# Routing weights spread in three transfers per half, and the last row's gate copies moved from the scalar to the vector engine

## The reference

```python
scores = sigmoid(xt @ gate_w.T)
_, idx = top_k(scores + gate_b, 4)
w = take_along_axis(scores, idx); w = w / sum(w) * 2.5
comb = zeros((T, 16)).at[arange(T)[:, None], idx].add(w)     # the routing weights
def expert_body(y, (w13_e, w2_e, c_e)):
    gate, up = split(xt @ w13_e.T)                            # 64 columns each
    return y + c_e[:, None] * ((silu(gate) * up) @ w2_e.T)
y = scan(expert_body, 0, (w13, w2, comb.T)) + shared_expert(xt)
x = layernorm(x + y)
```

## Time and profile before

| | |
|---|---|
| time, median of 3 runs | 1407.15 us (1401.17 to 1414.5) |
| the profiled execution | 1402.87 us |
| its span, first to last instruction | 1401.1 us |
| busy: DVE, PE, ACT, POOL | 995.9, 891.7, 561.5, 84.2 us |
| chain that ended last | DVE 36%, PE 26%, issue 14%, ACT 11%, DMA 8%, SPq 4% |
| of the chain, DMA big<-comb_rows | 3% |
| TensorE clock granted, mean | 0.783 of full speed |

### The profile page before, as it was taken

The page is one execution under the profiler, slowest core; times in us unless marked ns, Lnnn a source line. Parts: engine busy times, 40 slices in busy tenths (PEclk is TensorE's granted clock), DMA queues, the critical chain, the costliest instruction groups (busy, mean ns, idle before and its releaser), DMA issues.

```text
span 1401.1 us, 29222 instructions
## 1 busy us (share of the span) xinstructions
PE 891.7 (64%) x11808; PEld 538.8 (38%) x11808; DVE 995.9 (71%) x2294; ACT 561.5 (40%) x1259; POOL 84.2 (6%) x56
## 2 busy tenths in 40 slices
PE   4655756786467587787457586787457576471554
PEld 2433535454234254454224254454324254240122
DVE  5456563567699987576699987566699986344985
ACT  3232332555643332565642332555643331455310
POOL 0000000020000000020000000020000000030630
PEclk8656767699768789699768789688767788686897
DMA  4110010311222210311223210311232210302410
GB/s 144 32 39 18 25 40 11 69 36 36 71 75 77 69 32 18 69 36 35 71 76 77 68 32 18 62 36 36 72 75 77 69 32 10 68 1 62 118 63 8
DMA packets 84823, 72.20 MB, mean 52 GB/s; under 512 B 24528, under 2 KB 63440, under 8 KB 84496
## 3 DMA queue, kind: packets, MB, share of 16 engines
q1 hardware_dynamic: 84688, 70.34, 19.2%
HBM read 66.51 MB, written 3.80 MB: 50 GB/s over the span
## 4 chain that ended last, share of the span: by engine, by line
DVE 36%; PE 26%; issue 14%; ACT 11%; DMA 8%; SPq 4%; POOL 0%; DVEq 0%; POOLq 0%; ACTq 0%
PE bank L720 6%; DVE SG L1739 5%; DMA big<-comb_rows 3%; PE bank L547 3%; SPq L484 3%; PE bank L752 2%; DVE Y L1832 2%; DVE XP L1752 2%; PE bank L878 2%; ACT relu_s L1031 2%; DVE CV L1752 2%; DVE bank L1739 1%; DMA RB<-rows_bounce 1%; DVE ml L1472 1%; DVE big L1727 1%
## 5 line engine op out<-in xcount | busy, mean ns | idle before, releaser
L720 PE MATMUL bank<-onehot,tparts 128*32 128x256 bf16 x3840 | 136.9, 303 | 56.7 <-DVE onehot L1518 54.0
L720 PEld LDWEIGHTS bank<-onehot,tparts 128*32 128x32 bf16 x3840 | 111.2, 106 | 91.2 <-issue 81.2
L878 PE MATMUL bank<-XP,CO 128*128 128x512 f32 x128 | 82.7, 780 | 57.8 <-DVE XP L1750 33.3
L1739 DVE TENSOR_TENSOR_SCAN SG<-big 128x512 f32<-128x512 f32 x96 | 111.7, 1204 | 0.9
L1220 ACT ACTIVATE big<-DEL,Aneg 128x512 f32<-128x512 f32 x96 | 63.8, 715 | 100.8 <-DVE SG L1739 94.9
L878 PE MATMUL bank<-CV,CO 128*128 128x512 f32 x128 | 79.2, 750 | 34.8 <-DVE CV L1752 22.8
L1031 ACT ACTIVATE relu_s<-bank,nml 128x192 f32<-128x192 f32 (+1 forms) x128 | 52.8, 425 | 110.4 <-DVE nml L1477 110.4
L1472 DVE TENSOR_REDUCE ml<-bank 128x2 f32<-128x384 f32 (+1 forms) x64 | 33.7, 568 | 65.6 <-PE bank L655 34.9
L752 PE MATMUL bank<-GT,QBD 128*32 128x32 f32 x3072 | 56.2, 208 | 33.3 <-DVE G L1527 23.4
L1518 DVE TENSOR_SCALAR onehot<-ib,CO 128x1024 bf16<-128x1024 f16 x160 | 69.9, 480 | 10.3 <-PE bank L720 8.6
L1084 ACT ACTIVATE GT<-bank 128x256 f32<-128x256 f32 x64 | 24.5, 383 | 129.7 <-PE bank L720 129.6
(11 more groups left out here) (307 smaller groups left out, 1979.2 us busy)
## 6 DMA issues: line engine op xcount, KB each, us to landing
BC<-bc_rows SPq DMA_DIRECT2D x128, 256.0 KB, 4.2
ib<-idx_rows SPq DMA_DIRECT2D x64, 256.0 KB, 4.0
big<-comb_rows SPq DMA_DIRECT2D x8, 1024.0 KB, 9.9
rows_bounce<-RO SPq DMA_DIRECT2D x256, 8.5 KB
W<-w SPq DMA_DIRECT2D x1, 2818.0 KB, 15.3
RB<-rows_bounce SPq DMA_DIRECT2D x16, 136.0 KB, 2.1
X<-x SPq DMA_DIRECT2D x4, 256.0 KB, 2.8
out<-CV SPq DMA_DIRECT2D x4, 256.0 KB, 2.3
```

What stands on the lines that cost most here:

```text
L720: m = mm(bank[2 + c % 2][32 * bb:32 * bb + 32, 256 * kind:256 * kind + 256], tparts[:, kt, part, 32 * kind:32 * kind + 32], onehot[:, n % ...
L878: mm(bank[5 + j][:, :], ident, hC[(n - 1) % 2][:, j, :], start=(n == 1), stop=(n == DS)).then_inc(ysum.sem, ysum.up())
L1739: m = dve.tensor_tensor_scan(state, decay, dBu[:, n % 2, j, :], 0.0, ALU.mult, ALU.add)
```

## The change

The two loads of `CB` per row become six: for pairs 0 and 1 (both halves, 256 KB each), for pairs 2 and 3 (256 KB each), and for pairs 4 to 7 (512 KB each), in this order, with the same packets of 2 KB. Each of the three parts has its own semaphore. POOL waits at steps 1 and 2 for the first part, at 3 and 4 for the second, from 5 on for the third. In the last row alone, ACT no longer copies the gate to `GU_turn`; DVE does it, behind a wait for `gm_ok` (ACT's relu on the same bank) and, as ACT did, for `hu_ok` of the step that had the buffer.

```diff
--- before.py
+++ after.py
@@ -338,6 +338,8 @@
         ct_ps = signal("comb_t_in_psum", 1)
         ct_sb = signal("comb_t_in_sbuf", 1)
         ct_st = signal("comb_stored", 1, 16)
+        cb_first = signal("routing_weights_spread_first_pairs", 2, 16)
+        cb_next = signal("routing_weights_spread_next_pairs", 2, 16)
         cb_sb = signal("comb_spread", 2, 16)
         ga_ps = signal("gate_in_psum", 9)
         up_ps = signal("up_in_psum", 9)
@@ -499,9 +501,10 @@
                 sp.wait_ge(ct_sb.sem, ct_sb.at(b, 1))
                 sp.dma_start(comb_rows, CT[:, :]).then_inc(ct_st.sem, ct_st.up())
                 sp.wait_ge(ct_st.sem, ct_st.at(b, 1))
-                for e in range(2):
-                    src = comb_rows.rearrange("(p e) t -> e p t", e=2)[e].unsqueeze(0).to_broadcast([64, NE // 2, L])
-                    sp.dma_start(CB[64 * e:64 * e + 64, :, :], src).then_inc(cb_sb.sem, cb_sb.up())
+                for lo, hi, part in ((0, 2, cb_first), (2, 4, cb_next), (4, NE // 2, cb_sb)):
+                    for e in range(2):
+                        src = comb_rows.rearrange("(p e) t -> e p t", e=2)[e][lo:hi].unsqueeze(0).to_broadcast([64, hi - lo, L])
+                        sp.dma_start(CB[64 * e:64 * e + 64, lo:hi, :], src).then_inc(part.sem, part.up())
                 for _ in range(EXPERT_PHASES - 2 + NORM_PHASES + SCAN_IN_PHASES - 4):
                     yield
                 sp.wait_ge(xd_sb.sem, xd_sb.at(b, 1))
@@ -1156,9 +1159,10 @@
                     if k >= T:
                         act.wait_ge(sg_ok.sem, sg_ok.at(b, k - T + 1))
                     clamped(bank[k0][0:rows, :], SGk[0:rows, 0, :], gm_ok)
-                    if k >= 3:
-                        act.wait_ge(hu_ok.sem, hu_ok.at(b, k - 2))
-                    A(GU_turn[k % 3][0:rows, :], bank[k0][0:rows, :], ACT.Copy).then_inc(gx_ok.sem, gx_ok.up())
+                    if not alone:
+                        if k >= 3:
+                            act.wait_ge(hu_ok.sem, hu_ok.at(b, k - 2))
+                        A(GU_turn[k % 3][0:rows, :], bank[k0][0:rows, :], ACT.Copy).then_inc(gx_ok.sem, gx_ok.up())
                     yield
                     act.wait_ge(gm_ok.sem, gm_ok.at(b, k + 1))
                     sigmoid_logs(SGk[0:rows, 0, :])
@@ -1291,7 +1295,8 @@
                     yield
                 for k in range(1, 9):
                     pool.wait_ge(ga_used.sem, ga_used.at(b, k + 1))
-                    pool.wait_ge(cb_sb.sem, cb_sb.at(b, 2))
+                    spread = cb_first if k <= 2 else cb_next if k <= 4 else cb_sb
+                    pool.wait_ge(spread.sem, spread.at(b, 2))
                     GUk = GU_turn[k % 3]
                     pool.tensor_tensor(GUk, GUk, CB[:, k - 1, :], ALU.mult).then_inc(ht_ok.sem, ht_ok.up())
                     yield
@@ -1660,6 +1665,11 @@
                         hidden(k - lag)
                     if k >= 1:
                         yield
+                    if alone:
+                        dve.wait_ge(gm_ok.sem, gm_ok.at(b, k + 1))
+                        if k >= 3:
+                            dve.wait_ge(hu_ok.sem, hu_ok.at(b, k - 2))
+                        CP(GU_turn[k % 3][0:rows, :], bank[k0][0:rows, :]).then_inc(gx_ok.sem, gx_ok.up())
                     dve.wait_ge(gx_ok.sem, gx_ok.at(b, k + 1))
                     dve.wait_ge(up_ps.sem, up_ps.at(b, k + 1))
                     TT(GU_turn[k % 3][0:rows, :], GU_turn[k % 3][0:rows, :], bank[k0 + 1][0:rows, :], ALU.mult).then_inc(ga_used.sem, ga_used.up())
```

## The result

| | before | after |
|---|---|---|
| median, runs | 1407.07 us, 4 (1401.17 to 1414.5) | 1389.95 us, 4 (1385.9 to 1398.89) |
| ratio, 95% interval | | 0.989, 0.9849 to 0.993 |
| the profiled execution; its span | 1402.87; 1401.1 us | 1398.89; 1397.1 us |
| mean granted clock of it | 0.783 | 0.774 |

The changed kernel is faster by 1.1%. The forecast was 1390 us. Two later sets gave 1388.49 against 1406.18 and 1390.41 against 1402.74 us.

The account below looks back on a forecast made before the run. The prediction saw waits on each row's routing-weight loads, with ACT setting the pace afterwards in the last row. Gains of 11.0 us (last row) and 4.4 us (woven rows), 15.4 us from a level of 1405, gave 1390 us, range 1380 to 1402.

Parts of the forecast that it names:

- Step 1: Last row: first weights land 5.0 us after the first issue, so POOL starts 7.95 us sooner.
- Step 2: Last row: PE returns at full clock, POOL to relu of step 4 takes 5.12 us, gaining 1.85 us.
- rival B: Last row: the clock falls as before, so the kernel takes 1391.5 us; chance 0.10.
- Step 3: Last row: without the gate copy ACT's four steps shrink from 3.09 to 2.75 us each, gaining 1.37 us.
- Step 4: Last row's tail: last relu to `hidden(8)` takes 3.91 us instead of 3.70, a loss of 0.21 us.
- Step 5: Woven rows: `hidden(1)` starts sooner, then index load or PE limits; gains 1.7 + 1.8 + 0.9 = 4.4 us.
- Step 6: SP's queue: six issues cost about 2.7 us instead of 1.26, covered by the index store's wait for bytes ahead.
- A: Only the last row gains, a later wait swallowing the woven rows' 4.4 us; 1394 us, chance 0.19.
- C: The six transfers are served side by side, first part landing with the last; 1404 us, chance 0.06.
- D: SP's queue pays each transfer's fixed part in turn, delaying index loads 13 us; 1439 us, chance 0.04.
- E: Faster: the queue drains sooner with both halves written at once, and PE may keep its clock; 1386 us, chance 0.05.

Follow-up runs that it names:

- e3: Kernel before with only the last row's gate copy moved from ACT to DVE, two transfers as before; 1407.71 us against 1406.18, ratio 0.9996.
- e4: Changed kernel, but rows 0 to 2 load whole halves as before; split and DVE copy only in the last row; 1394.96 us, ratio 0.9916.
- e1: The changed kernel timed again without any edit; 1388.49 us against 1406.18, ratio 0.9847.
- e2: Changed kernel with six transfers, but the last row's gate copy back on ACT; 1394.33 us, ratio 0.9898.
- e5: Changed kernel plus four unused products on PE before `second(1)` of the last row; 1392.14 us against 1403.72, ratio 0.9899.
- e9: The changed kernel once more, unedited, beside three later kernels on the same chip; 1390.41 us against 1402.74, ratio 0.9903.
- e11: Changed kernel plus two, not four, unused products on PE before `second(1)` of the last row; 1391.79 us, ratio 0.9926.
- e6: e5 plus three unused PE products beside each woven expert stage, before the next row's first `pick`; 1382.69 us, ratio 0.9853.
- e10: Changed kernel plus three unused PE products beside each woven expert stage, none in the last row; 1387.42 us, ratio 0.9889.
- e12: Changed kernel with eight transfers in four parts, four semaphores, plus e10's added products in woven rows; 1386.64 us, ratio 0.9889.
- e8: Changed kernel with sixteen transfers of 128 KB, one semaphore per pair of experts; 1385.77 us, ratio 0.9871.
- e7: Changed kernel with the same six transfers issued in reverse order, pairs 0 and 1 last; 1402.88 us against 1403.72, ratio 0.9986.

## Why the prediction was right, step by step

Us after the row's store of `comb_rows`, means over woven rows (in profiles of whole halves: before, e3, e4; of six transfers in order without filler in woven rows: after, e1, e2, e5, e9, e11):

| | whole halves, 9 rows | six in order, 18 rows | reversed, 3 rows | filler (e6, e10), 6 rows |
|---|---|---|---|---|
| `hidden(1)` | 15.93 | 13.58 | 15.30 | |
| `onehots(0)` | 21.03 | 18.67 | 20.40 | 18.71 |
| first `pick` | 21.66 | 20.28 ± 0.13 | 21.02 | 19.33 ± 0.07 |
| `hidden(8)` | 68.14 | 67.10 ± 0.19 | 67.95 | 66.38 ± 0.43 |
| `ib` issued | 14.61 | 14.10 | | |

*Step 1, first weights.* Right: 5.18 us forecast as 5.1, against 13.06. Nearly all of the last row's gain is this.

*Step 2, the clock.* This failed. In the three profiles of the changed kernel (after, e1, e9) the clock fell 0.1, 1.3 and 0.5 us after PE had come back, and POOL to the relu of step 4 took 6.85, 5.76 and 6.56 us instead of 5.12; where that is less, the four steps behind took more than 11.01 (12.01 and 11.20), so that from POOL to `hidden(8)` all three took 21.7 to 21.8: rival B in its place. In e4, with the same last row, it did not fall (20.16); in e10, again with the same one, it did. What the prediction took from the earlier trace rows holds (full clock 2.5 to 4.5 us after PE's last product, 1220 to 1222), but it is one execution, and was read as more than it says. Length of the gap alone does not decide: the clock fell after gaps of 3.88, 3.04 (e1), 3.98, 4.01 (e10), 2.29 (e2) and 1.95 us (e11), and stayed after 3.69 (e4), 2.35 (e12) and 1.64 (e8). What else decides is open; the runs show only that the same instructions can meet either level. The section "What's actually happening" of "TensorE: Matmul & The Clock Gate" in the Trainium skill says that the window in which activity is judged runs freely, so that the same work varies from run to run; the rows here agree with that, and do not show the window.

*Step 3, the copy.* Right: relus 2.75 apart, DVE's copy 0.69 us for a forecast 0.67. By itself it is worth 1.0 us of the stage (e3, e2), net of step 4, for a forecast 1.16; from POOL's first product on, where the landing of the weights plays no part, 1.5 (e3) and 1.2 (e2).

*Step 4, the tail.* Right: 3.93 for 3.91.

The last row gained 9.1 us for a forecast 11.0, and step 2 is the difference.

*Step 5, woven rows.* The sum is right, the reason only in part. At the first `pick` they gain 1.38 each, 4.1 us in all, for 4.4. `hidden(1)` gained 2.35 for the 2.2. But in row 0 the limit was not the `ib` load. The prediction had it land 19.2 us after the store, from the 4.7 us of the earlier trace rows; in after it landed at 17.06, having been issued 0.8 us sooner and taken 3.3, and in no woven row of the changed kernel's three profiles later than 17.8. So `onehots(0)` gained all of its 2.36; PE, at 1.2 GHz over 282 to 284, was late instead, as it was forecast for rows 1 and 2. e10 shows it: with the clock up, `pick` came 1.0 sooner. Of the gain at `pick` 1.0 ± 0.3 per row, 3.1 us in all, is left at `hidden(8)`. How much reaches the next row is not resolved: from one row's store to the next it is 314.5 ± 0.9 us over the 18 rows, 315.4 ± 0.7 over the 9.

*Step 6, issuing.* The size was off: six issues took 3.84 us, not 2.7, at 0.6 each for 256 KB and 512 KB alike (1 MB: 0.63 in the earlier trace rows, 128 KB: 0.6 in e8). It stayed covered: the index store waits for the bytes ahead, and `ib` was issued no later.

*The rivals.* A: e4's times and the table, with 1.0 ± 0.3 us per woven row still there at `hidden(8)`, speak against it; neither settles it alone. B: happened in the last row. C: refuted by e7. D: refuted by e8. The Trainium skill's fixed 2.0 us per transfer ("DMA: Bandwidth & Descriptors", "Anatomy of one DMA"; given there for transfers issued from GpSimd, where here SP issues), if paid in turn, would by estimate have made e8's drain 14 x 2.0 = 28 us longer than that of two transfers; in the last row it was 0.3. E: the queue drains 0.4 to 0.8 us sooner (12.5 for 12.9 in the last row, 11.9 for 12.7 in row 0), and reversed, where nothing else can help, `pick` came 0.6 sooner than with whole halves. The other half of E came in some executions: in row 0 of e1 and e11, without filler there, PE waited 0.55 and 0.59 us for `onehots(0)` and the first `pick` came 19.3 us after the store; in the other four profiles with these woven rows PE was late. With filler it came in every woven row of e6 and e10.

*The sum.* Traces give 9.1 + 3.1 to 4.1 = 12.2 to 13.2 us. The means of the three sets of runs give 16.3 ± 4.2, 15.8 ± 2.1 and 13.3 ± 1.8. Whether the rest is more than the spread of runs isn't settled. The forecast's 15.4 lies in their middle, though 1.9 us of it, in the last row, did not come. That 1390 was met to 0.05 us is luck: the level before was 1407.07, 2.1 us above the 1405 put there, and the medians differ by 17.1 us, 1.7 more than the 15.4; the two cancel.

## What to carry to other kernels

When one bulk load feeds a loop, look which slice the first step needs, put that slice first in the queue under its own semaphore, and ask what will be late next: here 2 MB of load hid behind a 5 us first part without costing the queue anything. Within this queue the order and size of what stands ahead set a landing, not the count of transfers, as long as moving the bytes takes longer than issuing the loads (0.6 us each here). More parts are not free for sure: in one of the three woven rows of e12 the eight parts drained late and the index load with them; why is open. A term for an engine's clock after a gap belongs in the range, not in the sum.

## What the runs showed of the hardware

- **Issuing.** SP took 0.6 us to issue a load to 64 partitions, whether of 128, 256, 512 KB or 1 MB; a load to 128 partitions of 256 KB took 0.35 to 0.43.
- **Small transfers.** In the last row 2 MB in 16 transfers of 128 KB drained in 13.2 us, in 6 in 12.5, in 2 in 12.9. Each of the 16 landed 2.8 to 3.9 us after its issue.
- **POOL and DVE at once.** Of two products that meet, with all inputs in SBUF, the second to start is drawn out. In after, POOL's of 1223.52 took 1.26 us, and DVE's `hidden(1)`, begun 0.14 later, 1.67 instead of 0.69; at 1242.19 DVE came first with 0.68, and POOL's, begun 0.16 later, took 1.65 instead of 1.26. "GPSIMD Engine Reference" in the Trainium skill, section "Specifications", says that GpSimd shares its SBUF interfaces with VectorE and contends with its instructions of two SBUF inputs; these rows agree, and so does row 0 of after, where a DVE product with one input in PSUM began 0.15 us ahead of POOL's and both kept their times (0.69 and 1.27). In the last row it costs 1 us between the first weights and `second(1)`.
- **The clock.** After an idle 3.69 us PE came back at 2.4 GHz and kept it (e4); after an idle 1.95 us it was at 1.2 GHz 0.5 us later (e11). The same instructions met either level in different executions.
